# Exponents of four of sixteen heads moved to ScalarE in two cross attentions, an earlier start of a feed-forward, and an earlier first gather

## The chip, the cores and the metric

The kernel runs on one core of a Trainium2 chip. The core has five engines that run their own instruction queues and meet at semaphores: TensorE (PE in the profile, with its weight loads as PEld), VectorE (DVE), ScalarE (ACT), GpSimd (POOL) and SyncE (SP), which issues most of the DMAs. The metric is the time of one execution on the device in microseconds (us), median of the runs shown. All matrix products named below are float32.

## The reference, cut to what matters

The whole is two gated layers over 2 x 1024 tokens of 256 channels, with a context of 64 tokens for each of the two sequences. Layer 0 has a causal self attention and a cross attention, then two layers of local attention with a feed-forward behind each. Layer 1 has a cross attention and a mixture of 16 experts. The parts that the change touches are these:

```python
# cross attention 2 (16 heads of 32 channels) and 3 (16 heads of 16 channels), 64 context tokens
scores = jnp.einsum('bhqd,bhkd->bhqk', qh, kh) * scale
attn = jax.nn.softmax(scores, axis=-1)
out = jnp.einsum('bhqk,bhkd->bhqd', attn, vh)

# feed-forward behind each of the two local attentions (DEPTH = 2)
x = x + o @ wo
h = shift_token(x)                       # the later 128 channels come from the token before
h = (h - mu) / jnp.sqrt(var + 1e-05) * lg + lb
a, g = jnp.split(h @ w1 + b1, 2, axis=-1)
x = x + (a * gelu(g)) @ w2 + b2

# experts: the 128 tokens with the highest logits of each of 16 experts
_, idx = jax.lax.top_k(logits.T, top_k)
xe = xn[idx]
```

## The kernel before

The 2048 tokens are 16 tiles of 128 (`NT` = 16). Each engine has its own loop over `it`, with a fixed lead for each step; nothing but this written order and the semaphores sets who runs when.

**Cross attention** (`cross_attention`, lines 912 to 1309, run once as `x2` and once as `x3`). A tile has 16 heads x 64 context tokens = 1024 scores in each of 128 partitions, in PSUM (`sps`, two buffers of two banks). For tile t: TensorE's `score(t)` makes the scores; VectorE's `top(t)` takes the negative maximum of each head (`nmax`) and adds it to the scores, writing all 1024 columns to `prob` in SBUF; ScalarE's `exponent(t)` exponentiates `prob` in place in one instruction; VectorE's `shares(t)` sums and inverts; GpSimd's `share(t)` multiplies; TensorE's `turn_probs(t, half)` transposes half of the tile at a time into the one PSUM bank `tps`, ScalarE's `evacuate(t, half)` copies it out; TensorE's `weigh(t)` makes the outputs and ScalarE's `outputs(t)` copies them. `inputs` and `queries` are ScalarE's copies around the projection of the queries. The order of an iteration `it` (what is past its last tile drops out) is

- ScalarE: `evacuate(it-1, 0)`, `exponent(it+1)`, `outputs(it-2)`, `inputs(it+11)`, `evacuate(it-1, 1)`, `queries(it+7)`.
- TensorE: `turn_probs(it-1, 0)`, `turn_z(it+11)`, `project(it+7)`, `turn_probs(it-1, 1)`, `score(it+3)`, `weigh(it-1)`.
- VectorE: `shares(it)`, `top(it+2)`, then normalising and statistics of later tiles.

`score(t)` writes the buffer of tile t-2 and so waits for its reader: `pe.wait_ge(s.prob_ready, t - 1)`, which VectorE's addition of tile t-2 gives. `project` is asked in every iteration up to `it` = 8 in x2 (four blocks of channels), and in half of them, up to 6, in x3 (two blocks).

**Local attention and feed-forward** (`depth_layers`, lines 1386 to 1988), twice. Again a loop over tiles with leads, and behind it a loop over 4 groups of 4 tiles for the feed-forward, which TensorE fills. The first group needs its statistics (`early_half`, `late_half` on VectorE), `inverse_deviation` (GpSimd), `ffn_normalise` (VectorE), `turn` (TensorE, eight transposes) and `normed` (ScalarE) before TensorE's first `hidden`. In the kernel before these stand in the last two iterations of the loop and behind it: statistics at `NT - 2`, `inverse_deviation` behind GpSimd's loop, `ffn_normalise` at `NT - 1` behind `early_probs`, `turn` at `NT - 1` between `score` and `project_out`, `normed` behind ScalarE's loop. `outputs(it)` on VectorE (line 1591) copies the attention's result for `project_out` (line 1903), and `hidden` (line 1935) stands behind that.

**Experts.** A router block ends with the list of tokens `idxT` (line 2296). Then comes a barrier of all engines, and the next block begins with GpSimd's 16 gathers (line 2437), one for each expert, into `xe`; TensorE's `turn(0)`, `turn(1)` and `fc1(0)` follow in this order.

Of the kernel before, what the change touches and what calls it, by code (L numbers as in the profile page):

```python
# [9 lines left out]
def build(nc, io, out):  # L10
# [10 lines left out]
    P = 128  # L21
# [43 lines left out]
    with stack:  # L65
# [846 lines left out]
        def cross_attention(phase, H, DK, src, res, weights, affine, biases, scale, ahead):  # L912
# [10 lines left out]
            with ExitStack() as c:  # L923
# [22 lines left out]
                NPB = 4  # L946
                prob = sb(phase + "prob", [P, NPB, H * CT], F32, c)
# [12 lines left out]
                            "@p_turned @pT_done @pv_done @totalled @rinv_done @shared @out_done")  # L960
# [32 lines left out]
                with nc.Block() as block:  # L993
# [57 lines left out]
                    def _(dve):  # L1051
# [46 lines left out]
                        def top(t):  # L1098
# [3 lines left out]
                            if t >= NPB:  # L1102
                                dve.wait_ge(s.p_turned, 2 * (t - NPB) + 2)
                            dve.tensor_tensor(heads(prob[:, t % NPB, :]), heads(sps[t % 2][:]),
                                              nmax[:, t % 2, :].unsqueeze(2).to_broadcast([P, H, CT]),
# [29 lines left out]
                    def _(act):  # L1135
# [23 lines left out]
                        def exponent(t):  # L1159
                            act.wait_ge(s.prob_ready, t + 1)  # L1160
                            act.activation(prob[:, t % NPB, :], prob[:, t % NPB, :], ACT.Exp, scale=scale).then_inc(s.exp_done, 1)
# [49 lines left out]
                    def _(pe):  # L1211
# [67 lines left out]
                        def score(t):  # L1279
# [4 lines left out]
                            else:  # L1284
                                pe.wait_ge(s.prob_ready, t - 1)
# [100 lines left out]
        def depth_layers(weights, ffn_ahead, x3_ahead):  # L1386

            w1, w2, b1, b2, aff = weights
            with ExitStack() as c:
# [67 lines left out]
                with nc.Block() as block:  # L1457
# [21 lines left out]
                    def _(pool):  # L1479
# [51 lines left out]
                        for l in range(DEPTH):  # L1531
                            s, w = sa[l], sf[l]
                            pool.wait_ge(s.tab1, 6)
                            for it in range(-LEAD_X, NT):
                                if live(it + 1):
                                    scale(it + 1)
                                if live(it + LEAD_QK):
                                    sines(it + LEAD_QK)
                            inverse_deviation(w, 0)
# [7 lines left out]
                    def _(dve):  # L1547
# [130 lines left out]
                        for l in range(DEPTH):  # L1678
# [4 lines left out]
                            for it in range(-LEAD_X, NT):  # L1683
                                if live(it):
                                    early_probs(it)
                                if it == NT - 1:
                                    ffn_normalise(w, 0)
# [10 lines left out]
                                if it == NT - 2:  # L1698
# [3 lines left out]
                                if it == NT - 2:  # L1702
# [23 lines left out]
                    def _(act):  # L1726
# [61 lines left out]
                        for l in range(DEPTH):  # L1788
                            s, w = sa[l], sf[l]
                            for it in range(-LEAD_X, NT):  # L1790
                                if live(it):
# [11 lines left out]
                            act.wait_ge(w.w_in, 208)  # L1803
                            for g in range(G):
                                normed(w, g)
# [3 lines left out]
                    def _(pe):  # L1809
# [138 lines left out]
                        for l in range(DEPTH):  # L1948
                            s, w = sa[l], sf[l]
                            for it in range(-LEAD_X, NT):  # L1950
                                if live(it):
# [14 lines left out]
                                if it == NT - 1:  # L1966
                                    turn(w, 0)
# [61 lines left out]
        idxT = sb("idxT", [P, E], U32, moe)  # L2029
        RING = 4  # L2030
# [5 lines left out]
        with ExitStack() as c:  # L2036
# [49 lines left out]
            with nc.Block() as block:  # L2086
# [21 lines left out]
                def _(pool):  # L2108
# [16 lines left out]
                    for g in range(G):  # L2125
                        coefficients(g)
                        if g + 2 < G:
                            base(g + 2)

# [266 lines left out]
        with ExitStack() as c:  # L2396
            FC = FE // P
            xe = sb("xe", [P, E, ROW], F32, c)
# [227 lines left out]
```

## Time and profile before

| | |
|---|---|
| median of 3 runs | 2087.25 us (2085.36 to 2087.59) |
| the profiled execution | 2069.51 us, its span 2067.7 us |
| mean granted TensorE clock | 0.961 |
| PE busy | 1784.8 us, 86% |
| DVE busy | 1276.2 us, 62% |
| ACT busy | 1037.7 us, 50% |
| POOL busy | 697.6 us, 34% |
| HBM | 47 GB/s over the span |

The span runs from the first instruction to the last. Busy shares are averages over stages that have different limits, so what a change in a stage is worth has to be read in that stage: from the order of its instructions in time and from what each of them waited for.

### The profile page before, as it was taken

The numbers are of one execution on the slowest core, as the hardware profiler recorded it, in microseconds if no ns is written. First come the engines' busy times: TensorE is split into PE (matmuls) and PEld (weight loads), VectorE is DVE, ScalarE is ACT, GpSimd is POOL, SyncE is SP. The second block draws the span as 40 slices with busy tenths as digits, with TensorE's granted clock in tenths as the row PEclk, the third lists the DMA queues.
The fourth block names the chain that finished last, engine by engine and source line by source line (L and its number), as shares of the span: only waits on it lengthen the run. The fifth ranks groups of instructions, "written<-read, shape, count | busy, mean of one in ns | idle before, by whom it ended". The sixth has DMA issues, their size and how long they took to land. (4 is left out here: it accounts for less than half of the span.)

```text
span 2067.7 us, 32324 instructions
## 1 busy us (share of the span) xinstructions
PE 1784.8 (86%) x11428; PEld 1184.4 (57%) x11428; DVE 1276.2 (62%) x2721; ACT 1037.7 (50%) x2198; POOL 697.6 (34%) x1001
## 2 busy tenths in 40 slices
PE   6978888888799897998899989999998998872795
PEld 3455555555576555766566665556666555451795
DVE  5478888888733386233788863258887443878212
ACT  3488888888712165121676741147675211541222
POOL 0022223223324344242555541125555211550322
PEclk9999999999999999999999999999999999996898
DMA  3441111110000110020000002010000000028695
GB/s 120 155 130 42 42 42 42 42 42 2 1 1 1 31 32 1 0 63 28 17 6 5 3 6 67 0 44 1 6 6 6 20 0 16 1 68 222 179 310 166
DMA packets 104897, 101.71 MB, mean 49 GB/s; under 512 B 34896, under 2 KB 88481, under 8 KB 104609
## 3 DMA queue, kind: packets, MB, share of 16 engines
q1 hardware_dynamic: 101664, 95.31, 15.6%
q0 software_dynamic: 3072, 4.34, 1.2%
q8 instruction: 92, 1.51, 0.3%
q14 instruction: 69, 0.56, 0.1%
HBM read 80.60 MB, written 16.92 MB: 47 GB/s over the span
## 5 line engine op out<-in xcount | busy, mean ns | idle before, releaser
L586 DVE TENSOR_REDUCE negmax<-sps 128x1 f32<-128x1024 f32 x256 | 308.4, 1215 | 36.0 <-PE sps L531 31.5
L630 ACT ACTIVATE prob<-sps,negmax 128x1024 f32<-128x1024 f32 x256 | 287.4, 1122 | 21.6 <-DVE negmax L586 18.7
L540 PE MATMUL sps<-ident,prob 128*128 128x128 f32 x1152 | 177.8, 282 | 58.4 <-ACT prob L630 57.4
L540 PEld LDWEIGHTS sps<-ident,prob 128*128 128x128 f32 x1152 | 134.2, 143 | 143.1 <-ACT prob L630 124.0
L1504 POOL TENSOR_TENSOR la_pr<-la_pr,la_ri 128x512 f32<-128x512 f32 x128 | 157.1, 1256 | 163.1 <-DVE la_ri L1566 163.1
L675 POOL TENSOR_TENSOR probT<-probT,after 128x128 f32<-128x128 f32 x256 | 116.5, 455 | 268.0 <-DVE probT L594 192.4
L1753 ACT ACTIVATE la_pr<-la_pr,la_nx 128x256 f32<-128x256 f32 x256 | 126.3, 494 | 127.4 <-DVE la_nx L1607 127.4
L531 PE MATMUL sps<-ks,qs 128*128 128x512 f16 x512 | 160.8, 389 | 10.7 <-DVE ores L606 4.4
L1935 PE MATMUL la_bs<-lf_zT,lfw 128*128 128x512 f32 x352 | 153.0, 594 | 0.0
L1514 POOL TENSOR_TENSOR la_qs<-la_qn,ores 128x256 f32<-128x256 f32 x128 | 113.8, 921 | 88.8 <-DVE la_qn L1620 88.8
L639 ACT COPY probT<-sps 128x512 f32<-128x512 f32 (+1 forms) x192 | 101.7, 530 | 41.1 <-PE sps L540 41.1
L1935 PEld LDWEIGHTS la_bs<-lf_zT,lfw 128*128 128x128 f32 x352 | 66.4, 190 | 82.4 <-issue 82.3
L1877 PE MATMUL la_bqk<-ores,la_hT 128*128 128x512 f32 x224 | 104.0, 607 | 0.0
L1944 PE MATMUL la_bqk<-lfw,lf_hT 128*128 128x256 f32 (+1 forms) x384 | 95.4, 392 | 2.4 <-DVE lf_hT L1663 2.4
L1607 DVE CUSTOM_DVE_ANT_0 la_pr<-la_bs,la_mf 128x256 f32<-128x256 f32 x256 | 90.7, 418 | 10.6 <-PE la_bs L1894 10.5
L1820 PE MATMUL la_bs<-ident,la_pr 128*128 128x128 f32 x512 | 74.0, 291 | 24.5 <-POOL la_pr L1504 24.4
L1663 DVE SCALAR_TENSOR_TENSOR lf_hT<-la_bs,lfb,lf_gl 128x512 f32<-128x512 f32 (+1 forms) x48 | 36.0, 749 | 94.9 <-ACT lf_gl L1781 92.8
L594 DVE COPY probT<-sps 128x512 f32<-128x512 f32 (+3 forms) x192 | 91.9, 479 | 1.4 <-PE sps L540 1.4
L1781 ACT ACTIVATE lf_gl<-la_bs,lfb 128x512 f32<-128x512 f32 x40 | 27.5, 687 | 125.6 <-PE la_bs L1935 125.6
L1820 PEld LDWEIGHTS la_bs<-ident,la_pr 128*128 128x128 f32 x512 | 61.6, 149 | 49.3 <-POOL la_pr L1504 36.8
L1944 PEld LDWEIGHTS la_bqk<-lfw,lf_hT 128*128 128x128 f32 (+1 forms) x384 | 68.3, 189 | 29.8 <-issue 18.4
L563 PE MATMUL sps<-probT,vres 128*32 128x128 f32 x2304 | 78.9, 281 | 0.1
(374 smaller groups left out, 3722.6 us busy)
## 6 DMA issues: line engine op xcount, KB each, us to landing
w1e<-in_fc_T SPq DMA_DIRECT2D x16, 1024.0 KB, 5.9
w2e<-in_fc_T SPq DMA_DIRECT2D x16, 1024.0 KB, 8.7
qs<-q_parts SPq DMA_DIRECT2D x128, 64.0 KB, 1.9
ks<-k_parts SPq DMA_DIRECT2D x128, 64.0 KB, 2.0
q_parts<-parts SPq DMA_DIRECT2D x8, 512.0 KB, 4.0
k_parts<-parts SPq DMA_DIRECT2D x8, 512.0 KB, 3.6
lfw<-in_L_ffn_w SPq DMA_DIRECT2D x6, 640.0 KB
ores<-in_L_ffn_wqkv SPq DMA_DIRECT2D x2, 1536.0 KB, 6.4
```

The costliest lines, as they stand in the source:

```text
L531: mm = pe.matmul(slots[n % 4][:, half * 512:(half + 1) * 512], qs[:, buf, i * P:(i + 1) * P], ks[:, buf, half * 512:(half + 1) * 512], sta ...
L540: mm = pe.transpose(slots[n % 4][:, at * P:(at + 1) * P], prob[:, n % 3, t * P:(t + 1) * P], ident[:])
L586: dve.tensor_reduce(negmax[:, n % 4:n % 4 + 1], slots[n % 4][:], X, ALU.max, negate=True).then_inc(s.max_done, 1)
L630: act.activation(prob[:, n % 3, :], slots[n % 4][:], ACT.Exp, bias=negmax[:, n % 4:n % 4 + 1], accum_out=rowsum[:, tile % 2, n % QUAD:n % ...
L675: pool.tensor_tensor(blk, blk, after[:], ALU.mult).then_inc(s.masked, 1)
L1504: ins = pool.tensor_tensor(prob[:, h:h + 2, :], prob[:, h:h + 2, :], rinv[:, h:h + 2].unsqueeze(2).to_broadcast([P, 2, 2 * P]), ALU.mult)
L1514: pool.tensor_tensor(qs[:, q * HL:(q + 1) * HL, a * 32:(a + 1) * 32], qn[:, q * HL:(q + 1) * HL, (1 - a) * 32:(2 - a) * 32], sinr[:, t % T ...
L1753: ins = act.activation(prob[:, h, :], prob[:, h, :], ACT.Exp, scale=-1.0, bias=nmax[:, h:h + 1], accum_out=rsum[:, h:h + 1])
L1820: mm = pe.transpose(bs[:, half * 1024 + n * 256 + w * P:half * 1024 + n * 256 + (w + 1) * P], prob[:, h, w * P:(w + 1) * P], ident[:])
L1877: mm = pe.matmul(raw(t)[:, n * INNER:(n + 1) * INNER], shifted_rows(t, k), wqkv[:, k, n, :], start=(k == 0), stop=(k == KD - 1))
L1935: mm = pe.matmul(dst, w1[:, k, at:at + P], zT[:, k, :], start=(k == 0), stop=(k == KD - 1))
L1944: mm = pe.matmul(p3[j // 2][:, j % 2, :], uT[0:n, f, j * P:(j + 1) * P], w2[0:n, f, :], start=(f == 0), stop=(f == NF - 1))
```

## The change

In both cross attentions the last four of the sixteen heads (`HV` = 12 to 15) take another way: VectorE's addition covers the first 12 heads only; ScalarE first multiplies the four heads' `nmax` by the scale (a 128 x 4 instruction), exponentiates the 12 heads in place, and then exponentiates each of the four heads by an instruction of its own, from the scores in PSUM with the scaled maximum as bias. `score` of the tile after next now waits for `exp_done` in place of `prob_ready`.

Around the feed-forward, the first group's statistics move from `NT - 2` to `NT - 4`, `inverse_deviation` from behind the loop to `NT - 3`, `ffn_normalise` from `NT - 1` (behind `early_probs`) to `NT - 2` (ahead of it), `turn` to the head of TensorE's iteration `NT - 1`, and `normed` to the head of ScalarE's.

In the experts, `xe` becomes a view of `ores`, and the gather of expert 0 is issued at the end of the router block, ahead of the barrier; the other 15 stay where they were.

```diff
+                HA = 4
+                HV = H - HA
+                bias = sb(phase + "bias", [P, 2, HA], F32, c)
...
                         def top(t):
-                            dve.tensor_tensor(heads(prob[:, t % NPB, :]), heads(sps[t % 2][:]),
-                                              nmax[:, t % 2, :].unsqueeze(2).to_broadcast([P, H, CT]),
+                            dve.tensor_tensor(heads(prob[:, t % NPB, :])[:, 0:HV, :], heads(sps[t % 2][:])[:, 0:HV, :],
+                                              nmax[:, t % 2, 0:HV].unsqueeze(2).to_broadcast([P, HV, CT]),
                                               ALU.add).then_inc(s.prob_ready, 1)
...
                         def exponent(t):
                             act.wait_ge(s.prob_ready, t + 1)
-                            act.activation(prob[:, t % NPB, :], prob[:, t % NPB, :], ACT.Exp, scale=scale).then_inc(s.exp_done, 1)
+                            act.mul(bias[:, t % 2, :], nmax[:, t % 2, HV:H], scale).then_inc(s.bias_done, 1)
+                            act.activation(prob[:, t % NPB, 0:HV * CT], prob[:, t % NPB, 0:HV * CT], ACT.Exp, scale=scale)
+                            act.wait_ge(s.bias_done, t + 1)
+                            for h in range(HV, H):
+                                ins = act.activation(prob[:, t % NPB, h * CT:(h + 1) * CT], sps[t % 2][:, h * CT:(h + 1) * CT], ACT.Exp,
+                                                     scale=scale, bias=bias[:, t % 2, h - HV:h - HV + 1])
+                            ins.then_inc(s.exp_done, 1)
...
                         def score(t):
-                                pe.wait_ge(s.prob_ready, t - 1)
+                                pe.wait_ge(s.exp_done, t - 1)
```

GpSimd in `depth_layers`:

```diff
                             for it in range(-LEAD_X, NT):
+                                if it == NT - 3:
+                                    inverse_deviation(w, 0)
...
-                            inverse_deviation(w, 0)
```

VectorE in `depth_layers`:

```diff
+                                if it == NT - 2:
+                                    ffn_normalise(w, 0)
                                 if live(it):
                                     early_probs(it)
-                                if it == NT - 1:
-                                    ffn_normalise(w, 0)
...
-                                if it == NT - 2:
+                                if it == NT - 4:
                                     early_half(w, 0)
...
-                                if it == NT - 2:
+                                if it == NT - 4:
                                     late_half(w, 0)
```

ScalarE in `depth_layers`:

```diff
+                                if it == NT - 1:
+                                    act.wait_ge(w.w_in, 208)
+                                    normed(w, 0)
                                 if live(it):
                                     late_probs(it)
```

TensorE in `depth_layers`:

```diff
+                                if it == NT - 1:
+                                    turn(w, 0)
                                 if live(it):
                                     turn_probs(it)
...
-                                if it == NT - 1:
-                                    turn(w, 0)
```

GpSimd, at the end of the router block and in the expert block:

```diff
+                    pool.wait_ge(s.idx_done, 1)
+                    pool.wait_ge(s.rows_out, 16 * G)
+                    pool.indirect_dma_start(out=xe[:, 0, :], out_offset=None, in_=token_rows,
+                                            in_offset=bass.IndirectOffsetOnAxis(ap=idxT[:, 0:1], axis=0)).then_inc(x_in[0], 16)
...
-                    for e in range(E):
+                    for e in range(1, E):
```

## Rows read from the trace of the kernel before

**Rows 1.** Windows: stretch, length; busy us and instructions of each engine; granted clock; DMA.

```profile
757.46:792.12 34.66, 34.62 (x314) 24.12 (x312) 29.64 (x34) 23.43 (x42) 16.00 (x16) 1.00 0.00 1
792.12:817.76 25.64, 18.22 (x208) 14.02 (x208) 18.93 (x21) 15.02 (x24) 11.67 (x13) 1.00 0.00 1
1786.64:1807.77 21.13, 19.61 (x178) 12.08 (x176) 20.17 (x23) 14.34 (x27) 10.94 (x12) 1.00 0.00 1
1807.77:1836.70 28.93, 20.83 (x240) 13.84 (x240) 26.33 (x30) 18.32 (x33) 15.57 (x16) 1.00 0.01 1
```

**Rows 2.** Timeline, x2: start, us, engine, line, operation, tiles, count, idle before.

```profile
764.44 0.82 ACT L1176 ACTIVATE x2xT<-x2z_ps,x2aff 128x128 f32<-128x128 f32 x2
...
792.60 1.06 ACT L1161 ACTIVATE x2prob<-x2prob 128x1024 f32<-128x1024 f32 x1
...
793.41 1.16 PE L1289 MATMUL x2s<-x2kblk,x2qT 64*128 64x128 f32 x16
793.56 0.58 ACT L1166 COPY ores<-x2o_ps 128x512 f32<-128x512 f32 x1
...
794.03 0.60 ACT L1157 COPY x2pT<-x2t_ps 128x512 f32<-128x512 f32 x1
794.68 1.09 PE L1274 MATMUL x2o_ps<-x2pT,x2vblk 128*64 128x128 f32 x16
...
796.39 0.58 ACT L1157 COPY x2pT<-x2t_ps 128x512 f32<-128x512 f32 x1 [1.77 <-PE x2t_ps L1238]
```

**Rows 3.** Timeline, x3, one iteration of its second half.

```profile
1812.67 1.13 PE L1289 MATMUL x3s<-x3kblk,x3qT 64*128 64x256 f32 x8
1812.83 0.36 ACT L1166 COPY ores<-x3o_ps 128x256 f32<-128x256 f32 x1
1813.08 0.60 ACT L1157 COPY x3pT<-x3t_ps 128x512 f32<-128x512 f32 x1
...
1813.74 0.65 PE L1274 MATMUL x3o_ps<-x3pT,x3vblk 128*32 128x128 f32 x16
1814.31 0.66 PE L1238 MATMUL x3t_ps<-ident,x3prob 128*128 128x128 f32 x4
```

**Rows 4.** Groups by shape, ScalarE, whole span: busy, mean ns, idle before.

```profile
L1744 ACT ACTIVATE la_nm<-la_ss 128x16 f32<-128x16 f32 x32 | 6.4, 201 | 5.7 <-DVE la_ss L1597 5.7
```

**Rows 5.** Timeline, ScalarE, experts: eight instructions with a bias from PSUM.

```profile
1932.68 2.17 ACT L2504 ACTIVATE hTe<-bh,b1e 128x128 f32<-128x128 f32 x8 [9.44 <-PE bh L2529]
```

**Rows 6.** Timeline, last two iterations of the first local attention, start of its feed-forward.

```profile
1214.95 1.23 DVE L1570 COPY la_pT<-la_bs 128x1024 f32<-128x1024 f32 x1 [2.58 <-PE la_bs L1820]
...
1217.92 1.97 PE L1853 MATMUL la_bv<-la_pT,la_v 128*64 128x128 f32 x32
...
1230.78 2.27 PE L1853 MATMUL la_bv<-la_pT,la_v 128*64 128x128 f32 x32
...
1234.07 0.68 DVE L1591 COPY la_oT<-la_bv 128x512 f32<-128x512 f32 x1
...
1235.14 1.89 PE L1903 MATMUL la_bz<-ores,la_oT 128*128 128x256 f32 x8
...
1236.87 8.32 PE L1935 MATMUL la_bs<-lf_zT,lfw 128*128 128x512 f32 x19
```

**Rows 7.** Timeline, the same place in the second layer.

```profile
1616.07 0.69 DVE L1591 COPY la_oT<-la_bv 128x512 f32<-128x512 f32 x1 [0.51 <-PE la_bv L1853]
...
1617.03 1.89 PE L1903 MATMUL la_bz<-ores,la_oT 128*128 128x256 f32 x8
```

**Rows 8.** Tile of the normalised rows: duration min/median/max ns, first and last start.

```profile
L1653 DVE TENSOR_SCALAR lf_z<-x0res,lf_mom,lf_rs x32: 334/340/765, 1230.3 to 1703.2; 128x128 f32<-128x128 f32 x32
```

**Rows 9.** Windows, as in Rows 1, a stretch of the second layer's last iteration.

```profile
1610.40:1612.30 1.90, 1.86 (x8) 1.57 (x8) 0.96 (x2) 0.00 (x0) 1.82 (x3) 0.50 0.00 0
```

**Rows 10.** Timeline, the first two gathers of the experts.

```profile
1922.75 1.24 POOL L2437 DMA_INDIRECT xe<-token_rows,idxT  x1 [52.79 <-POOLq L42]
1924.29 0.97 POOL L2437 DMA_INDIRECT xe<-token_rows,idxT  x1 [0.30 <-issue]
```

More of the change, by code:

```diff
@@ L959, in cross_attention @@
                             "@x_rstd @z_done @z_turned @xT_done @q_done @qT_done @scores @max_done @prob_ready @exp_done "
-                            "@p_turned @pT_done @pv_done @totalled @rinv_done @shared @out_done")
+                            "@p_turned @pT_done @pv_done @totalled @rinv_done @shared @out_done @bias_done")
                 ZPAIR = LEAD_X - 1 if MC == J else 0
@@ L1802, in _ @@
                                     values(it + LEAD_QK)
-                            act.wait_ge(w.w_in, 208)
                             for g in range(G):
-                                normed(w, g)
+                                if g > 0:
+                                    normed(w, g)
                                 gelus(w, g)
@@ L2029, in build @@
         idxT = sb("idxT", [P, E], U32, moe)
+        xe = ores[:].rearrange("p a n -> p (a n)")[:, 0:E * ROW].rearrange("p (e c) -> p e c", c=ROW)
+        x_in = [nc.alloc_semaphore(f"e_x_in{i}") for i in range(E)]
         RING = 4
@@ L2397, in build @@
             FC = FE // P
-            xe = sb("xe", [P, E, ROW], F32, c)
             xeT = sb("xeT", [P, 2, D], F32, c)
@@ L2413, in build @@
             w_in = (s.w_in0, s.w_in1, s.w_in2, s.w_in3)
-            x_in = [nc.alloc_semaphore(f"e_x_in{i}") for i in range(E)]
             with nc.Block() as block:
```

## The prediction

> **What bounds the kernel now.** I read the page first. TensorE is busy for 86% of the span, so the first question in each changed stage is whether TensorE is what it waits for. That I read from windows cut at the starts of ScalarE's copy `evacuate(t, 0)`, one per tile, and then from the timeline inside them.
>
> In x2's first half (seven tiles, 34.66 us, 4.95 a tile) TensorE is busy for 34.62 of 34.66 us: it is the bound. In x2's second half (six tiles, 4.27 each) it is busy for 18.22 of 25.64 us, and VectorE for 18.93: neither is full. In x3, five tiles take 21.13 us (4.23 each) with both near full, and the last eight take 28.93 (3.62 each), VectorE 26.33, TensorE 20.83 [rows 1]. The timeline says what fills the second halves. Two engines hand one PSUM bank to and fro: ScalarE's first copy starts at 792.12, its exponent 0.48 later at 792.60, `outputs` 0.96 later, the second copy 0.47 later; 0.65 after that TensorE's `weigh` can start, and weighing and the next tile's first transposes lead 1.71 later to the next first copy at 796.39 [rows 2]. The sum, 0.48 + 0.96 + 0.47 + 0.65 + 1.71 = 4.27, is the whole period. In x3 the same ring is 0.48 + 0.96 + 0.25 + 0.66 + 0.57 + 0.70 = 3.62, again the whole period (the 0.70, transposes to copy, is the remainder) [rows 1, 3]. The exponent stands in this ring; VectorE's addition does not. ScalarE is half idle, but its idle time is behind the ring's TensorE part, where the exponent, in queue order, can't go.
>
> **Cross attention, the cost.** VectorE loses 256 of the 1024 columns of the addition. Its copies out of PSUM take 1.23 us for 1024 columns and 0.68 for 512 [rows 6]; by their slope, (1.23 - 0.68) / 512 = 1.07 ns a column, that is 0.27 us. It is off the ring: worth nothing.
>
> ScalarE's exponent gets one small multiplication, 768 columns and four times 64 columns. The next instruction starts 0.96 after the old exponent [rows 2], so 768 columns are 0.72 (three quarters). The multiplication is as small as the 128 x 16 root, 0.20 long [rows 4], of which 0.10 overlaps as with the exponent (1.06 long, next after 0.96): 0.10. The trace has no 64-column exponent. From above, the eight 128-column instructions with a bias from PSUM take 2.17 together, 0.26 each with the overlap [rows 5]; from below, the 128 x 16 root steps in about 0.10 [rows 4]. 64 columns fewer at 0.94 ns save 0.06 from the 0.26: I take 0.21 and 0.32 for the last to its end. So the exponent occupies 0.10 + 0.72 + 4 x 0.21 = 1.66 before the next instruction, against 0.96: +0.71. It is done after 0.10 + 0.72 + 3 x 0.21 + 0.32 = 1.78, against 1.06. The wait for `bias_done` costs nothing: 0.72 of exponent lies between.
>
> The page ScalarE: Activation LUTs of the Trainium skill (What ACT_TABLE_LOAD costs) gives 280 ns plus 0.833 ns a column with a pointer bias, 93 ns of it overlapped. That would be an estimated 0.24 a piece, so 0.12 a tile more, and 128 columns would step by 0.29, where this trace shows 0.26.
>
> The second cost is the new gate. `score(t)` now waits for the exponent of tile t-2, and `weigh` is queued behind it, on which ScalarE's and VectorE's next steps hang. First copy to exponent 0.48, exponent done 1.78, handing over 0.05, scoring 1.09 (1.16 less 0.07 of overlap), then 1.71: 5.11 in x2 [rows 2]; in x3 0.48 + 1.78 + 0.05 + 1.06 + 0.57 + 0.70 = 4.64 [rows 3]. The first ring becomes 4.27 + 0.71 = 4.98 in x2, with the two input copies (0.82 less 0.10 of overlap, so 0.70 as they follow one another [rows 2]) 5.68; in x3 4.33, with inputs about 4.60. The longer ring sets the tile:
>
> - x2, first seven: three with inputs 5.68, four gated 5.11: 37.5 against 34.66, +2.8.
> - x2, last six: four gated 5.11, two without a score 4.98: 30.4 against 25.64, +4.8.
> - x3, first five: 4.64 each: 23.2 against 21.13, +2.1.
> - x3, last eight: six at 4.64, two at 4.33: 36.5 against 28.93, +7.6.
> - Run-up of the first two tiles: the first scores gated, mostly behind other work: +0.4 together, bounds 0 and 3.
>
> Together +17.7 us. TensorE is not slowed by waiting more, I assume: its granted clock stayed 1.00 over x2's last six tiles with 18.22 us busy of 25.64 [rows 1].
>
> **Feed-forward, the gain.** In the first layer `weigh` of the last tile ends at 1230.78 + 2.27 = 1233.05, but VectorE, held by `ffn_normalise`, copies its output only at 1234.07; `project_out` starts at 1235.14 and `hidden` at 1236.87, 1.73 later. With normalising, transposes and ScalarE's copies gone ahead, the copy starts at 1233.1, `project_out` at about 1233.85, `hidden` at 1235.6: -1.3 [rows 6]. In the second layer the copy was at 1616.07 with `project_out` at 1617.03, held by the transposes; now 1616.8: -0.2 [rows 7]. The transposes fall into TensorE's wait for the last tile's probabilities. What moves in: statistics two iterations earlier lie beside ScalarE's exponents. `ffn_normalise`, eight instructions, goes ahead of `early_probs` of tile 14, which waited 2.58 us. Alone they take 0.34 each, beside GpSimd up to 0.77 [rows 8], so 2.1 to 5 us; I take 4, and `early_probs` ends 1.7 later than its 1216.18 (1214.95 + 1.23), still at the 1217.92 at which `weigh` takes it [rows 6]. If it is 5, and GpSimd's multiplications are held too, a layer loses up to 1 us; bound from below, no loss. Trainium Architecture — The Big Picture of the Trainium skill (What this means for kernel authors) calls the port that VectorE and GpSimd share an exclusive lock; the 0.77 beside 0.34 agrees, and by it the loss would be the larger one.
>
> TensorE's clock was at 0.50, its 1.2 GHz level, in part of these iterations after waits for the probabilities [rows 9]; eight transposes inside the wait may shorten or shift that. `weigh` took 2.27 for the last tile of the first layer, against 1.97 for the tile before [rows 6]. I take 0 and keep -1.7 to +1.5 a layer for the range. Sum of the part: -1.5, bounds -5 and +3.5.
>
> **First gather, nothing.** Behind the barrier gather 0 stands at 1922.75 and gather 1 at 1924.29 [rows 10]. TensorE's queue holds `turn(1)` ahead of the first `fc1`, so gather 1 counts, which stays behind the barrier, and GpSimd now comes to that barrier an issue (1.0 to 1.24) later. That uses up what the saved issue (1.54 from gather 0 to 1) gives: 0, bounds -1 and +1.
>
> **Sum.** +17.7 - 1.5 + 0 = +16.2. The profiled execution, 2069.51, becomes 2085.7. It stands 17.7 below the median, 2087.25; carried over to it, 2103.4.
>
> **Rivals.**
> - *VectorE is the bound after all, and is relieved.* It is busy for 26.33 of 28.93 us in x3's last eight tiles [rows 1], and the same engine stands at most tiles' ends. If tiles followed it, 32 tiles save 0.27 each, 8.6 us, and with the feed-forward the time is 2077. Against it: the ring adds up to the period to 0.01 in both attentions, and ScalarE's copy shows a wait of 1.77 for TensorE in every period [rows 2]. It would decide only if ScalarE's step grew by less than nothing on the ring. The Trainium skill's Perfetto Trace Analysis (Optimizing Scalar/DVE Operations) advises moving work from a saturated VectorE to ScalarE; by that this rival is the forecast. The rows show VectorE busy, not saturated.
> - *The small exponents are nearly free, and the feed-forward pays in full.* At 0.11 a piece the step grows by 0.31; the attentions cost about 8, and 5 come back in the feed-forward: +3, 2090, within 0.2%. The nearest row, at 0.26, speaks against.
> - *They don't overlap.* At 0.38 a piece (0.32 and a gap) the exponent grows by another 0.68 on some 26 tiles: 2121. The eight in 2.17 us speak against.
> - *TensorE's clock falls in the attentions*, as it waits more. Scoring, weighing and transposing are 2.3 us of x3's ring, which would be 4.6; over the last eight tiles of each attention alone that is some 40 us: 2140. For it: [rows 9]; against: the full clock in all four stretches of [rows 1].
>
> **How the numbers follow.** A change under 0.2%, about 4.2 us, can't be told from none. I give the forecast's mechanism 0.79 (between small exponents of 0.15 and 0.30 it spans 2095 to 2113), VectorE relieved 0.08, nearly free 0.07, no overlap 0.03, the clock 0.03. Range 2092 to 2113: the forecast's span and part of the nearly free case. Faster 0.08, same 0.07, slower 0.85.
>
> **What would show it.** Right: `exponent` of a tile from first start to last end about 1.8; periods of 5.1 in x2 and 4.6 in x3's second halves; `score` waiting for ScalarE; VectorE with more idle time. In the feed-forward: `hidden` starting 1.7 after a `project_out` that waits for nothing but the copy, and `early_probs` of tile 14 in time. Gather 1 as far behind the writing of `idxT` as before. Wrong would be: 64 columns in 0.1 or 0.4 us; unchanged periods; a granted clock below 1.00 in the attentions.

## The result and the profile after

The changed kernel took 2112.86 us (median of 4 runs, 2111.34 to 2113.23) beside 2086.36 for the kernel before on the same chip (2085.36 to 2087.59): a ratio of 1.0135, interval 1.0111 to 1.0160 (the quotient of the two medians is 1.0127). It is slower by 26.5 us by the medians. The direction is as forecast; the size is not (+16.2, a ratio of 1.0078). 2112.86 lies at the top of the range; the ratio laid on the 2087.25 from which the forecast started gives 2115.4, above it.

The page of the changed kernel, its first lines:

```profile
span 2111.4 us, 32485 instructions
## 1 busy us (share of the span) xinstructions
PE 1810.4 (86%) x11428; PEld 1200.4 (57%) x11428; DVE 1268.7 (60%) x2721; ACT 1059.6 (50%) x2358; POOL 698.8 (33%) x1001
```

The windows of the changed kernel, cut at the first copies of the same tiles as in [rows 1], and under them two windows at half the clock, one just behind the second stretch and one across the end of the fourth (columns as there; the granted clock stands behind the last engine's count):

```profile
758.75:796.57 37.82, 35.34 (x314) 24.34 (x312) 26.35 (x32) 27.96 (x77) 15.50 (x16) 1.00 0.01 2
796.57:829.60 33.03, 20.98 (x208) 16.09 (x208) 17.63 (x21) 19.24 (x54) 12.97 (x13) 0.87 0.00 0
...
1798.62:1822.22 23.60, 19.82 (x178) 12.46 (x176) 19.02 (x23) 17.56 (x51) 11.09 (x11) 1.00 0.00 1
1822.22:1866.73 44.51, 29.29 (x240) 18.68 (x240) 25.68 (x30) 23.95 (x72) 16.85 (x18) 0.76 0.00 1
...
830.00:841.00 11.00, 7.16 (x44) 5.29 (x44) 0.00 (x0) 3.51 (x7) 0.00 (x0) 0.50 0.01 1
...
1860.00:1875.00 15.00, 10.08 (x83) 6.06 (x72) 1.57 (x3) 5.89 (x15) 4.09 (x4) 0.50 0.01 1
```

The prediction had 37.5, 30.4, 23.2 and 36.5 us for these four stretches. Two came out (37.82, 23.60), at a clock of 1.00. The other two, 33.03 and 44.51, are the two in which the granted clock is below 1.00. The same 240 matmuls of x3's last eight tiles are 29.29 us busy, where they were 20.83 in [rows 1].

The ring of x2 in the changed kernel, that is the closed chain of steps of ScalarE and TensorE from one tile's first copy to the next tile's, to be laid beside [rows 2]:

```profile
801.77 0.59 ACT L1160 COPY x2pT<-x2t_ps 128x512 f32<-128x512 f32 x1 [1.99 <-PE x2t_ps L1247]
802.25 0.21 ACT L1164 ACTIVATE x2bias<-x2nmax 128x4 f32<-128x4 f32 x1
802.36 0.83 ACT L1165 ACTIVATE x2prob<-x2prob 128x768 f32<-128x768 f32 x1
...
803.09 0.92 ACT L1168 ACTIVATE x2prob<-x2s,x2bias 128x64 f32<-128x64 f32 x4
803.88 0.61 ACT L1175 COPY ores<-x2o_ps 128x512 f32<-128x512 f32 x1
...
804.15 1.16 PE L1298 MATMUL x2s<-x2kblk,x2qT 64*128 64x128 f32 x16 [1.03 <-ACT x2prob L1168]
...
805.25 1.09 PE L1283 MATMUL x2o_ps<-x2pT,x2vblk 128*64 128x128 f32 x16
...
806.96 0.59 ACT L1160 COPY x2pT<-x2t_ps 128x512 f32<-128x512 f32 x1 [1.99 <-PE x2t_ps L1247]
```

The exponent's step is 803.88 - 802.25 = 1.63 (forecast 1.66), its end 803.09 + 0.92 - 802.25 = 1.76 after its start (forecast 1.78). `score` stands at 804.15, waiting for ScalarE's exponent, as forecast; handing over takes 0.14, not 0.05. The period is 0.48 + 1.76 + 0.14 + 1.10 + 1.71 = 5.19 against a forecast of 5.11; in x3 it is 4.72 against 4.64. The chain is right to 0.08 a tile.

The same ring in x3, one iteration at the full clock and the next at half:

```profile
1836.94 1.13 PE L1298 MATMUL x3s<-x3kblk,x3qT 64*128 64x256 f32 x8 [1.02 <-ACT x3prob L1168]
1838.00 0.65 PE L1283 MATMUL x3o_ps<-x3pT,x3vblk 128*32 128x128 f32 x16
...
1839.27 0.59 ACT L1160 COPY x3pT<-x3t_ps 128x512 f32<-128x512 f32 x1 [1.73 <-PE x3t_ps L1247]
...
1841.66 2.08 PE L1298 MATMUL x3s<-x3kblk,x3qT 64*128 64x256 f32 x8 [1.03 <-ACT x3prob L1168]
...
1843.66 1.08 PE L1283 MATMUL x3o_ps<-x3pT,x3vblk 128*32 128x128 f32 x16
...
1845.53 0.59 ACT L1160 COPY x3pT<-x3t_ps 128x512 f32<-128x512 f32 x1 [3.27 <-PE x3t_ps L1247]
```

What changes is TensorE's part: scoring 1.13 becomes 2.08, weighing 0.65 becomes 1.08, and the next first copy comes 3.87 after `score` instead of 2.33. The periods of x3's last eight tiles (from first copy to first copy) are 6.26, 6.07, 4.72, 6.26, 6.07, 4.71, 5.22, 5.20: on and off, not steadily.

The feed-forward's start, both layers of the changed kernel ([rows 6, 7] before):

```profile
1247.95 2.27 PE L1866 MATMUL la_bv<-la_pT,la_v 128*64 128x128 f32 x32
1251.01 1.99 PE L1916 MATMUL la_bz<-ores,la_oT 128*128 128x256 f32 x8 [0.79 <-DVE la_oT L1601]
1252.84 3.60 PE L1948 MATMUL la_bs<-lf_zT,lfw 128*128 128x512 f32 x8
...
1627.04 2.27 PE L1866 MATMUL la_bv<-la_pT,la_v 128*64 128x128 f32 x32
...
1630.10 1.99 PE L1916 MATMUL la_bz<-ores,la_oT 128*128 128x256 f32 x8 [0.79 <-DVE la_oT L1601]
```

The first gather (before: [rows 10], with `idxT` written at 1920.91 and ScalarE's first instruction behind the barrier at 1921.96):

```profile
1954.32 0.17 DVE L2315 CAST idxT<-r_lgps 128x16 uint32<-128x16 f32 x1 [0.70 <-PE r_lgps L2410]
1954.79 1.24 POOL L2146 DMA_INDIRECT ores<-token_rows,idxT  x1 [52.83 <-DVE idxT L2315]
1958.96 1.28 ACT L2521 ACT_TABLE_LOAD   x1 [46.09 <-PEq L42]
...
1959.61 0.97 POOL L2454 DMA_INDIRECT ores<-token_rows,idxT  x1 [3.58 <-POOLq L42]
```

One kernel's executions differ by a stage or two, so the comparison below is with a second profiled execution of the kernel before, 2085.83 us, near its median, and not with the 2069.51 of the prediction. Its span is 2084.1, the changed kernel's 2111.4: +27.3. Stages are cut at the first or last instruction on a tile; "x2's tiles" reach from the first to the last transposes of its probabilities, "between" from there to the first ones of x3, "experts" from the first to the last `fc1`; 30.2 to 30.4 us follow in every row.

| us | start to x2's tiles | x2's tiles | between | x3's tiles | to `idxT` | to first `fc1` | experts |
|---|---|---|---|---|---|---|---|
| before, the prediction's | 750.8 | 71.8 | 956.0 | 62.5 | 79.6 | 6.9 | 109.8 |
| before, again | 748.5 | 75.9 | 960.5 | 62.5 | 79.7 | 6.9 | 119.8 |
| changed | 752.9 | 83.6 | 956.3 | 80.0 | 81.5 | 8.6 | 118.2 |
| attention alone | 751.0 | 83.8 | 959.6 | 83.9 | 81.3 | 6.9 | 120.3 |
| attention, TensorE filled | 753.2 | 81.5 | 960.7 | 71.8 | 78.0 | 6.9 | 111.1 |
| best | 750.6 | 70.2 | 952.4 | 62.4 | 79.5 | 6.9 | 118.7 |

### The profile page after: what moved, and what is told of

It is laid out like the page before. It is cut to its first block and busy times, and to the rows that moved or that the text cites. A ratio compares the mean times of both kernels' runs of the same rounds, so it can differ in the third digit from the quotient of the medians.

```text
span 2111.4 us, 32485 instructions
## 1 busy us (share of the span) xinstructions
PE 1810.4 (86%) x11428; PEld 1200.4 (57%) x11428; DVE 1268.7 (60%) x2721; ACT 1059.6 (50%) x2358; POOL 698.8 (33%) x1001
## 5 line engine op out<-in xcount | busy, mean ns | idle before, releaser
L586 DVE TENSOR_REDUCE negmax<-sps 128x1 f32<-128x1024 f32 x256 | 308.5, 1215 | 36.5 <-PE sps L531 31.9
L563 PE MATMUL sps<-probT,vres 128*32 128x128 f32 x2304 | 79.5, 283 | 0.1
```

Of the source, the lines that this page charges most:

```text
L586: dve.tensor_reduce(negmax[:, n % 4:n % 4 + 1], slots[n % 4][:], X, ALU.max, negate=True).then_inc(s.max_done, 1)
```

## The experiments

Twelve runs. The ratio is always to runs of the kernel before on the same chip, with its 95% interval; it differs from the quotient of the medians by up to 0.13%. For scale, 0.1% is 2.1 us.

**The kernel before once more** (`before_again`), unedited, for a second look at its stages.

> The kernel before, unchanged, to see what its own profile gives a second time. Its timed runs were 2085 to 2088, its profiled one 2069.5. If that one lacked something that the others have (a half-clock stretch, or the stretch near 1973 us of the changed kernel in which TensorE's instructions come 0.7 us apart), this profile shows it and takes about 2086; if the profiled execution is always faster, it is again near 2069.

Measured: 2085.41, ratio 0.9995 (0.9980 to 1.0010). The profiled execution is 16.4 us longer in span than the one that the prediction used: 4.1 in x2's tiles, 4.5 between the attentions, 10.0 in the experts' stage, less 2.3 ahead of x2's tiles. Its windows at the end of x2:

```profile
805.00:815.00 10.00, 6.42 (x56) 4.62 (x56) 5.93 (x8) 5.14 (x9) 4.09 (x4) 0.76 0.00 0
815.00:825.00 10.00, 7.65 (x46) 5.44 (x42) 0.00 (x0) 2.84 (x6) 2.04 (x2) 0.50 0.01 2
```

In this execution the kernel before has half the clock at x2's end too: its last three tiles take 4.97, 5.61 and 5.55, where the execution of [rows 1] had 4.27, 4.27 and 3.75, at 1.00. So the row from which I argued that the clock stays up told of that one execution: of the five profiled executions in which x2 is unchanged (these two, `ffn_alone`, `gather_alone` and `two_gathers`), four end it at half the clock, with one tile of 5.38 to 5.62 and a last one of 5.54 or 5.55.

**The change in three parts**, each alone on the kernel before: the exponents with the gate, the feed-forward, the gather (`attention_alone`, `ffn_alone`, `gather_alone`). Their edits are the pieces of the diff above: in `top`, `exponent` and `score`; in `depth_layers`; at the router's end.

> Only the exponents of four heads, their bias and the gate of score on the exponent; feed-forward and gather as before. Theory (the ring of ScalarE and TensorE grows by 0.71 to 0.8 us a tile, and TensorE's clock falls because it waits more): +24 to +30 over before, x2 tiles of 5.19 us at full clock, and half-clock stretches in both attentions. Rival (only the ring): +18 to +20, clock 1.00 in both.

> Only the earlier statistics, normalising, transposes and copies of the first feed-forward group. Theory: hidden starts 1.1 to 1.3 us earlier in the first layer and 0.2 to 2.9 in the second (the clock's part): -1.5 to -4. Rival (the trace's -2.9 in the second layer came from the shifted clock, not from the edit): -1 to -1.6.

> Only the first gather ahead of the barrier. Theory (the barrier waits until the gather has landed): the first instruction behind the barrier 4.4 us after idxT is written against 1.05 before, gather 1 1.7 us later, +1.7 to +2. Rival (the late gathers also starve TensorE's instruction fetch, as between 1973 and 1981 us of the changed kernel): +6 to +9, with TensorE's instructions 0.7 us apart during the second expert.

Measured: attention 2118.05, 1.0154 (1.0125 to 1.0183); feed-forward 2086.66, 0.9994 (0.9969 to 1.0019); gather 2086.73, 1.0006 (0.9987 to 1.0024). The loss is all in the attentions, and more than the forecast's 17.7 us for them (0.0154 x 2086 = 32), and a little more than the 24 to 30 expected. Its periods in x3 are 6.20, six of 4.72, and then 6.28, 5.79 and three of 6.56. The other two parts can't be told from nothing when alone. For the gather that speaks against the +6 to +9 of its rival; the late instructions on which that rival rested stand in the kernel before as well (last section).

**The gate alone, and the cut of the exponent alone**: what each does to the ring.

```diff
 # gate_alone, in score(t)
-                                pe.wait_ge(s.prob_ready, t - 1)
+                                pe.wait_ge(s.exp_done, t - 1)
 # split_alone, in exponent(t), VectorE still adding all 1024 columns
-                            act.activation(prob[:, t % NPB, :], prob[:, t % NPB, :], ACT.Exp, scale=scale).then_inc(s.exp_done, 1)
+                            part = prob[:, t % NPB, 0:12 * CT]
+                            act.activation(part, part, ACT.Exp, scale=scale)
+                            for h in range(12, 16):
+                                part = prob[:, t % NPB, h * CT:(h + 1) * CT]
+                                ins = act.activation(part, part, ACT.Exp, scale=scale)
+                            ins.then_inc(s.exp_done, 1)
```

> The kernel before with one line of the change: score of tile t waits for the exponent of tile t-2 in place of VectorE's addition; the exponent itself stays one instruction. Theory (both costs lie in the ring): first copy 0.48 + exponent done 1.06 + handing over 0.14 + score 1.10 + 1.71 = 4.49 us a tile in x2's second half against 4.27, and 4.0 against 3.62 in x3's: +3 to +5 in all, more only if the clock falls. Rival (the gate is hidden behind the other ring, the exponent's length alone costs): 0 to +1.

> The kernel before with the exponent in five instructions, 768 columns and four times 64, all in place in SBUF without bias; VectorE adds all 16 heads and the gate stays at its addition. Theory: ScalarE's step grows from 0.96 to about 1.4, so x2's second half goes to 4.7 a tile and x3's to 4.05, +8 to +10 over all, plus up to 8 if TensorE's clock falls. Rival (VectorE sets the tiles): 0 to +1.

Measured: gate 2083.24, 1.0013 (0.9984 to 1.0041), with second-half periods of 4.49 in x2 and 4.02 in x3 where 4.27 and 3.62 were; cut 2087.43, 1.0042 (1.0012 to 1.0071), with 4.64 and 3.98. Both costs show in the ring, each small by itself; in the changed kernel the periods are 5.19 and 4.72, more than both together: behind the gate the exponent's later end, 1.76 in place of 1.06, comes in whole (4.49 + 0.70 = 5.19). The gate alone can't be told from nothing in the time. Each of the two also has 0.50 for x3's last three tiles, 4.36, 4.65 and 4.65 with the gate and 4.86, 4.88 and 4.65 with the cut, where the unchanged kernel had 3.61, 3.61 and 3.30 at 1.00 in both of its profiles. The small pieces of the cut kernel, by groups of ScalarE, and those of the changed kernel, by line:

```profile
L1165 ACT ACTIVATE x2prob<-x2prob 128x64 f32<-128x64 f32 x64 | 10.9, 244 | 0.0
```

```profile
L1168 ACT ACTIVATE x2prob<-x2s,x2bias x64: 297/320/372, 747.5 to 825.2; 128x64 f32<-128x64 f32 x64
```

From SBUF with no bias tile a 64-column exponent is 0.24 long, from PSUM with one 0.32. In the changed kernel they step by about (803.88 - 803.09) / 4 = 0.20, near the 0.21 taken, while the rule of the Trainium skill's ScalarE: Activation LUTs (What ACT_TABLE_LOAD costs) gave an estimated 0.24.

**The four small exponents first**, and the gate on them alone, with the 768 columns behind.

```diff
                             act.mul(bias[:, t % 2, :], nmax[:, t % 2, HV:H], scale).then_inc(s.bias_done, 1)
-                            act.activation(prob[:, t % NPB, 0:HV * CT], prob[:, t % NPB, 0:HV * CT], ACT.Exp, scale=scale)
                             act.wait_ge(s.bias_done, t + 1)
...
-                            ins.then_inc(s.exp_done, 1)
+                            ins.then_inc(s.small_done, 1)
+                            act.activation(prob[:, t % NPB, 0:HV * CT], prob[:, t % NPB, 0:HV * CT], ACT.Exp,
+                                           scale=scale).then_inc(s.exp_done, 1)
 # in score(t)
-                                pe.wait_ge(s.exp_done, t - 1)
+                                pe.wait_ge(s.small_done, t - 1)
```

> The attention part alone, but the four heads' exponents go ahead of the 768 columns and score waits for them only. Theory: the gate's ring falls to about 4.6 (x2) and 4.1 (x3), the other ring of 0.96 + 0.67 + the uncovered wait for the bias (0.1 to 0.2) is left: 5.0 to 5.1 and 4.4 to 4.5 a tile against 5.19 and 4.73, so 3 to 5 less than the attention part alone, more if the clock holds. Rival (the gate costs nothing beside the exponent's length): 0, or +2 for the uncovered wait.

Measured: 2093.30, 1.0077 (1.0048 to 1.0105). TensorE in x2 of this kernel:

```profile
802.93 0.63 PE L1248 MATMUL x2t_ps<-ident,x2prob 128*128 128x128 f32 x4 [0.77 <-ACT x2pT L1160]
804.00 1.16 PE L1299 MATMUL x2s<-x2kblk,x2qT 64*128 64x128 f32 x16 [0.43 <-ACT x2prob L1167]
805.60 1.09 PE L1284 MATMUL x2o_ps<-x2pT,x2vblk 128*64 128x128 f32 x16 [0.44 <-ACT x2pT L1160]
```

The 1.03 us wait before `score` is now two of 0.43 and 0.44. The period falls only from 5.19 to 5.11 in x2 and from 4.72 to 4.45 in x3, but x3 keeps 4.45 up to its last three tiles: 72.0 us of tiles, 8.0 fewer than the changed kernel. The shorter ring is in eight of them, 8 x 0.27 = 2.2; the rest, 5.8, is the clock, since those eight held 1.00 where four of the changed kernel's took 6.07 to 6.26. Nothing fills TensorE's waits here; in x3 they are 0.77, 0.43 and 0.25 a tile. In x2 the clock fell all the same in the last three tiles (6.05, 6.46, 5.55). The time came down by more than the 3 to 5 us expected, but part of that is not this edit: in this profile the experts' stage is the short one (109.6, see the last section).

**The clock itself.** The attention part, with transposes of the identity into a PSUM bank that nothing reads at this point (`zps`): four behind the first transposes of a tile, six behind the second. They are added work and nothing else.

```diff
+                        def fill(n):
+                            for _ in range(n):
+                                pe.transpose(zps[:, 0:P], ident[:], ident[:])
...
+                                if it >= 6:
+                                    fill(4)
...
+                            if it >= 6 and live(it - 1):
+                                fill(6)
```

> The attention part alone, and from iteration 6 on ten extra transposes of the identity a tile on TensorE into a PSUM bank nobody reads, placed in its two waits of a tile. Theory (the clock's fall is the second cost): granted clock 1.00 through both attentions, and 8 to 14 us less than the attention part alone (2118), so 2104 to 2110, with the same 5.2 and 4.7 us a tile. Rival (the half-clock stretches cost little, as the ring waits for ScalarE anyway): 2116 or more, the fill only lengthens it.

Measured: 2093.08, 1.0060 (1.0034 to 1.0087), against 1.0154 without the fill (each to its own chip): 0.94%, some 20 us, come back for added work, where 8 to 14 were expected. By stages of the two profiles it is 2.3 in x2's tiles, 12.1 in x3's and 3.3 in the router, 17.7 together; the shorter experts' stage (111.1 against 120.3) is no part of it. Its windows in x3 and TensorE in one iteration:

```profile
1841.00:1851.00 10.00, 8.60 (x91) 6.70 (x90) 7.24 (x9) 6.54 (x20) 4.36 (x5) 1.00 0.01 2
1851.00:1861.00 10.00, 7.50 (x81) 5.67 (x79) 5.16 (x7) 6.95 (x24) 4.09 (x4) 1.00 0.01 2
1861.00:1870.00 9.00, 6.54 (x84) 4.99 (x84) 1.29 (x2) 3.80 (x9) 2.04 (x2) 1.00 0.00 0
```

```profile
1845.54 0.63 PE L1247 MATMUL x3t_ps<-ident,x3prob 128*128 128x128 f32 x4 [0.33 <-ACT x3pT L1160]
1846.00 0.82 PE L1306 MATMUL x3z_ps<-ident 128*128 128x128 f32 x6
1847.19 1.13 PE L1298 MATMUL x3s<-x3kblk,x3qT 64*128 64x256 f32 x8 [0.37 <-ACT x3prob L1168]
```

The granted clock is 1.00 to the end, `score` takes 1.13, and the waits of 0.77 and 1.02 have become 0.33 and 0.37. x3's periods are 4.72, but for the first (5.02), one of 5.47, and 4.31, 4.31 and 3.30 at the end; its tiles take 71.8 us, where attention alone took 83.9. In x2 the fill costs three tiles 0.75 each, where TensorE had no slack. This is the experiment that decides: the attention's own instructions and its ring are the same, and the time above the forecast goes with the clock.

**The exponent off the ring.** On the kernel before, the exponent of the next tile is issued behind the second copy instead of between the two.

```diff
-                            if live(it + 1):
-                                exponent(it + 1)
...
+                            if live(it + 1):
+                                exponent(it + 1)
```

> The kernel before with one move on ScalarE in the cross attentions: exponent(it+1) stands behind the second copy instead of between the two. Theory (the exponent costs only because it stands between the two copies): the ring of x2's second half falls from 4.27 to 3.70, then VectorE's 3.86 a tile is the bound; x3's stays at VectorE's 3.6 to 3.75. -2 to -4 in all. Rival (VectorE or GpSimd wait for the later exponent): tiles of 4.3 and more, 0 or slower.

Measured: 2076.84, 0.9950 (0.9931 to 0.9969), some 10 us where 2 to 4 were expected.

```profile
794.69 1.16 PE L1289 MATMUL x2s<-x2kblk,x2qT 64*128 64x128 f32 x16
794.79 0.58 ACT L1157 COPY x2pT<-x2t_ps 128x512 f32<-128x512 f32 x1 [0.32 <-PE x2t_ps L1238]
...
795.27 1.06 ACT L1161 ACTIVATE x2prob<-x2prob 128x1024 f32<-128x1024 f32 x1
...
795.78 1.09 PE L1274 MATMUL x2o_ps<-x2pT,x2vblk 128*64 128x128 f32 x16
```

`weigh` now follows `score` directly. x2's last tiles take 4.10 and at the end 3.75, 3.75, 3.75 at the full clock; x3's stay at 3.62. The 4.10 is above the 3.86 of VectorE that was expected as the next bound. x2's tiles take 70.2 against 75.9, of which 3.8 is half clock that doesn't occur here. ScalarE does the same work; its place in the queue is what changed.

**Fill on the kernel before** (four transposes from iteration 9 on, three more from iteration 13; same function as above).

> The kernel before, and from iteration 9 on four extra transposes of the identity in TensorE's wait for the first copy, three more in the last tiles ahead of weigh. Theory (the half clock at the end of x2 costs the kernel before some 3.6 us in those of its executions that have it): x2's last three tiles at 4.27, 4.27, 3.75 in the profile, -1 to -4 in the median. Rival (nothing to gain, as the clock holds anyway): 0.

Measured: 2080.88, 0.9973 (0.9956 to 0.9989). x2's tiles are at 71.7, with 4.28, 4.27 and 3.75 at the end. The kernel before itself loses about 4 us to the clock there (75.9 against 71.7) in an execution like its second one; the rest of the 5.6 us of the ratio isn't placed.

**Best**: the exponent behind the second copy, this light fill, and the feed-forward part of the change; nothing of the four heads, nothing of the gather.

> The kernel before with the feed-forward part of the change, the exponent behind the second copy and the fill in the last tiles. Theory: the three gains add: -2.5, -2, -1.5, so -4 to -8 against before, the version that beats both. Rival (each drowns in where the half-clock stretches fall): -2 to +2.

Measured: 2071.68 (2070.86 to 2072.68), 0.9920 (0.9904 to 0.9937), some 16 us less than the kernel before, where 4 to 8 were expected, and so faster than both. The three gains don't simply add: the exponent behind the second copy already ends x2 at the full clock, and x2's tiles take 70.2 with the fill and without. What the feed-forward part adds would be between the attentions, 952.4 against 955.9 with the exponent alone, by one profile each.

**Two gathers ahead of the barrier** on the kernel before, to see what the barrier waits for.

```diff
+                    for e in range(2):
+                        pool.indirect_dma_start(out=xe[:, e, :], out_offset=None, in_=token_rows,
+                                                in_offset=bass.IndirectOffsetOnAxis(ap=idxT[:, e:e + 1], axis=0)).then_inc(x_in[e], 16)
...
-                    for e in range(E):
+                    for e in range(2, E):
```

> The gather part alone, with gathers 0 and 1 both ahead of the barrier. Theory (the barrier opens when the last gather ahead of it has landed): ScalarE's first instruction behind the barrier 5.6 to 5.9 us after idxT is written (4.5 with one gather, 1.05 with none), turn(1) waits for no transfer, and the first fc1 starts 7.2 to 7.6 after idxT, between the 6.9 of before and the 8.6 of one gather. Rival (the barrier costs a fixed 3.4 more once there is a gather ahead of it, whatever its landing): ScalarE's first instruction at about 4.5 plus at most one issue less its overlap, the first fc1 at 6.5 or less.

```profile
1927.31 0.17 DVE L2303 CAST idxT<-r_lgps 128x16 uint32<-128x16 f32 x1 [0.70 <-PE r_lgps L2398]
1927.78 1.24 POOL L2134 DMA_INDIRECT ores<-token_rows,idxT  x1 [51.27 <-DVE idxT L2303]
1929.32 0.97 POOL L2134 DMA_INDIRECT ores<-token_rows,idxT  x1 [0.30 <-issue]
1933.28 1.28 ACT L2509 ACT_TABLE_LOAD   x1 [47.43 <-PEq L42]
```

Measured: 2087.02, 1.0001 (0.9983 to 1.0019). From the end of the cast to the first instruction behind the barrier it is 1.05 us with no gather ahead, 4.47 with one (1958.96 - 1954.49) and 5.80 with two. One issue more is 1.54; the other 1.9 of the first step is no issue. The barrier opens 4.17 after the first gather's start with one, and 3.96 after the second's start with two: it waits for the last one's transfer. The profile has the first gather landed 3.1 us after its issue and the second 2.8, so that the barrier opens 1.1 and 1.2 behind the landing, as it opens 1.05 behind the cast where no gather stands ahead. The first `fc1` starts 7.2 after `idxT`, as expected (7.2 to 7.6; 6.5 or less if the barrier's extra cost were fixed).

## Why the prediction fell short

**The ring of ScalarE and TensorE: right.** The place (exponent between the two copies, `score` gated), the small exponents (0.20 a step, 0.21 taken), the exponent's end (1.76, 1.78 forecast), and VectorE's relief being worth nothing all came out. Only the handing over was 0.14 for 0.05. The argument for the ring was weaker than it read: steps cut from one first copy to the next add up to the period whatever holds them, so the agreement to 0.01 shows nothing. What shows the ring is the wait of each engine for the other, and now the cut (+0.37 and +0.36 a tile) and the gate (+0.22 and +0.40). At the full clock the tiles take 81.5 less 2.3 of fill = 79.2 in x2 and 71.8 in x3 (with 0.8 of fill), where the forecast's terms give 71.8 + 7.6 = 79.4 and 62.5 + 9.7 = 72.2.

**TensorE's clock: wrong, and the step that failed.** "TensorE is not slowed by waiting more, I assume" put the clock at nothing, and was argued from stretches that had waits enough but showed 1.00 in the one execution that I had. The new ring adds a wait of 1.03 a tile before `score` to the 0.77 before the second transposes, and over x3's last eight tiles TensorE has its lower level, 1.2 GHz, in about half of the time: 44.51 us instead of 36.5, or 8.0, of which 7.6 is the clock, as the same tiles of the filled kernel take 36.9 at 1.00. Another 1.8 is in the router behind it (81.5 against 79.7; its first 9.6 us have a clock of 0.67 against 0.82, and with 1.00 in the filled kernel the router takes 78.0), which goes with the clock but was not separated. The rival of the falling clock, with 0.03 and +40 us on top, had the mechanism and not the size: it took all of the last eight tiles of both attentions at half clock, at 2.3 us a tile, where a tile of x3 wholly at half clock takes 6.56, or 1.84 more. That the time still came to the top of the range is luck: the range was made of small exponents of 0.15 to 0.30, which came out at 0.20, and had no clock of the attentions in it. The Trainium skill, TensorE: Matmul & The Clock Gate (A second HAM failure mode: psum-queue depth-cycling), tells of a kernel whose TensorE idles briefly and often between groups of matmuls and swings between the two levels; this trace agrees, with 0.76 over 44.51 us. I had not weighed it. In x2 the clock costs 4.1 us over the last three tiles (5.93 + 6.31 + 5.55 against 4.98 + 4.98 + 3.75), but the kernel before pays 3.8 at the same place in its second execution, so that x2 comes to +7.7 against it, beside +7.6 forecast.

**The sum**, changed kernel less the second execution of the kernel before: x2's tiles +7.7 (forecast 7.6), x3's +17.5 (9.7), router +1.8 (0), run-ups of x2 and x3 1.3 each, +2.6 (0.4), all other between the attentions -5.5 (-1.5), gather +1.7 and experts -1.6 (0), and +3.1 ahead of x2's first instruction, which the change can't have made: that stretch ends between 718.5 and 723.1 over the kernels of this study, whatever their edit. Together +27.3, 11.1 above the forecast's 16.2, 9.6 of it in x3 and the router.

**The feed-forward: mechanism right, the second layer mis-sized.** `project_out` waits 0.79 for VectorE's copy and nothing else, and `hidden` follows 1.83 later (1.7 forecast). From the last transposes' start to `hidden` the first layer went from 9.85 to 8.63 (-1.2, forecast -1.3). The second went from 10.31 to 8.43, where -0.2 was forecast: of these 1.9 us, 1.4 are `weigh`, which was 3.68 long at the half clock before and is 2.27 now. That was the term "I take 0" for the clock. The -0.2 itself came of that one execution. In the second one `weigh` of this layer is 2.27 long already, and TensorE then waits for the normalising as in the first layer:

```profile
1619.26 2.27 PE L1853 MATMUL la_bv<-la_pT,la_v 128*64 128x128 f32 x32
1622.61 1.09 PE L1924 MATMUL la_bqk<-ident,lf_z 128*128 128x128 f32 x8 [1.08 <-DVE lf_z L1655]
```

The long `weigh` had hidden this wait. Against the second execution the two layers go from 9.84 and 9.85 to 8.63 and 8.43. In `ffn_alone` both take 9.23, with `weigh` at 2.85 and 3.06: the edit saves the wait there too, and the clock takes about half of it back.

Normalising held VectorE for 4.14 us in the first layer (4 taken): its instructions took up to 1.08 while GpSimd's multiplications ran and 0.33 behind them, and `weigh` of tile 14 waited 0.17 for `early_probs`. From the transposes of tile 14 to its `weigh` it is 4.67 against 4.71 before, so nothing was lost. In the time the part doesn't show: alone it is 0.9994, its "between" 962.1 against 960.5 without it, and the intervals of 1.0154 (attention alone) and 1.0135 (with feed-forward and gather) overlap.

**The gather: nothing in the sum, by wrong reasons.** The barrier isn't one issue later but one transfer: 3.4 us. Gather 1, which was to stand as far behind the writing of `idxT` as before, starts 5.12 after it instead of 3.38. Ahead of the first `fc1` that leaves 8.6 - 6.9 = +1.7; gather alone shows the same 8.6, and an experts' stage of 118.8. The experts' stage is shorter by 1.0 to 1.6 in both, which fits weights that have had longer to arrive; that was not tested. The ratio of the gather alone is 1.0006.

**VectorE relieved, nearly free, no overlap:** none of them. VectorE's addition fell to 0.96 us, and every period grew.

## What to carry over

Find the ring that sets the period and put each edit on it or off it; an engine that is half idle has no free place for work if its in-order queue puts that work between two steps of the ring. The same exponent, moved behind the second copy, was worth 0.5%, part of it clock, and cutting it up in place cost 0.4%.

When an edit adds waits to TensorE inside a ring, price its clock as well, from more than one execution of the kernel: a granted clock of 1.00 in one profile doesn't say that there is room left. A few transposes into an unused bank tell within one run how much of a loss is clock.

Take two profiles of the kernel before where a few microseconds matter; here two of them differed by 16 us of span, more than the effect that was forecast.

## What the chip showed that was not expected

- The granted clock falls in a ring whose waits are 0.77 and 1.03 us in every tile, and comes back after a tile or two (periods 4.71, 6.26, 6.07, 4.72), though the tiles that kept it are the same instructions with the same waits. What decides between them is open; that filled waits keep it up is shown in both attentions, and that shorter ones do in x3 alone, each by one profile.
- A barrier at the end of a block of GpSimd's opens only when its gathers have landed: 1.05, 4.47 and 5.80 us for none, one and two.
- The experts' stage of the unchanged kernel takes 109.8 or 119.8 us. In the longer one single instructions of the second matmul come late, with no wait that the profile can name; TensorE in that execution:

```profile
1943.98 0.38 PE L2538 MATMUL by<-w2e,hTe 128*128 128x256 f32 x1 [1.15 <-issue]
1945.43 0.38 PE L2538 MATMUL by<-w2e,hTe 128*128 128x256 f32 x1 [1.07 <-issue]
1946.15 0.47 PE L2538 MATMUL by<-w2e,hTe 128*128 128x256 f32 x1 [0.34 <-issue]
```

The four kernels timed together on one of the chips all had the shorter stage in their profiles (109.6 to 111.1), and the eight of the two other sets all the longer one (118.7 to 120.3), which is why only ratios on one chip are compared here. That doesn't remove it: on the chip of those four, 10 of 31 runs of the unchanged kernel took 2068.4 to 2071.1 and the others 2075.9 to 2089.4. Small ratios there (the gate, the cut) are to be read with that. The cause of the two lengths was not sought.
